# An adaptive layer-norm block on one core: W_up turned by VectorE and DMAs in place of TensorE, the first modulation's columns made directly, and some copies moved between engines

## The reference

```python
mod = (silu(c) @ wmod).reshape(4, 6, 1, 512)       # sa, ca, ga, sb, cb, gb
ga, gb = sign(ga) * max(abs(ga), 0.25), the same of gb
h = layernorm(x) * (1 + ca) + sa
q, k, v = split(h @ Wqkv + bqkv)                   # 512 -> 3 x 128
x = x + ga * (softmax(q k^T / sqrt(128)) v @ Wo + bo)
h = layernorm(x) * (1 + cb) + sb
top1 = argmax(h @ gate_w^T + expert_bias)
ffn = h @ W_up^T + lora_B[top1] @ (lora_A[top1] @ h)
out = x + gb * ffn
```

## Time and profile before

| | |
|---|---|
| median of 3 runs | 181.64 us (181.44 to 181.71) |
| the profiled execution: its own time | 181.46 us |
| its span, first to last instruction | 179.7 us |
| granted TensorE clock, mean | 1.000 |
| busy: TensorE / its weight loads | 170.8 us (95%) / 134.0 us (75%) |
| busy: VectorE / ScalarE / GpSimd | 139.4 (78%) / 90.1 (50%) / 80.4 us (45%) |
| share of the last-ending chain: PE / DVE / POOL / ACT / issue / DMA | 68 / 10 / 7 / 6 / 5 / 2% |
| W_up's 16 transposes on TensorE (L658) | 1.91 us busy |
| W_up's high parts on ScalarE (L932), low parts on VectorE (L1303), 4 each | 2.06 us, 2.48 us |

### The profile page before, as it was taken

The page is one execution under the profiler, slowest core; times in us unless marked ns, Lnnn a source line. Parts: engine busy times, 40 slices in busy tenths (PEclk is TensorE's granted clock), DMA queues, the critical chain, the costliest instruction groups (busy, mean ns, idle before and its releaser), DMA issues.

```text
span 179.7 us, 2828 instructions
## 1 busy us (share of the span) xinstructions
PE 170.8 (95%) x918; PEld 134.0 (75%) x918; DVE 139.4 (78%) x352; ACT 90.1 (50%) x170; POOL 80.4 (45%) x109
## 2 busy tenths in 40 slices
PE   6889999989999999999999999999999999999990
PEld 5755757878678788878867787888887878768890
DVE  1957859998969997969999839699298275989964
ACT  3375045964278894339349651713477502583100
POOL 3464201279334549041979950019694000452550
PEclk9999999999999999999999999999999999999999
DMA  4999997930041002353031753001140000001414
GB/s 160 378 387 387 387 387 145 385 106 9 0 168 71 0 2 73 96 125 122 0 117 58 201 136 75 0 0 58 60 158 22 0 2 0 0 4 58 175 48 185
DMA packets 13902, 21.32 MB, mean 119 GB/s; under 512 B 3340, under 2 KB 4112, under 8 KB 13888
## 3 DMA queue, kind: packets, MB, share of 16 engines
q1 hardware_dynamic: 13888, 21.15, 35.3%
HBM read 14.83 MB, written 4.21 MB: 106 GB/s over the span
## 4 chain that ended last, share of the span: by engine, by line
PE 68%; DVE 10%; POOL 7%; ACT 6%; issue 5%; DMA 2%; SPq 0%; POOLq 0%; DVEq 0%; ACTq 0%
PE bank L398 44%; PE bank L412 3%; PE bank L521 3%; DVE stats L1020 2%; PE bank L548 2%; DMA xs<-in_L_attn_x_dram 2%; PE bank L506 2%; ACT xn_p L845 2%; PE bank L500 2%; PE bank L572 2%; PE bank L574 2%; PE bank L503 2%; POOL rstd L1493 1%; POOL xs L1508 1%; DVE xs L1232 1%
## 5 line engine op out<-in xcount | busy, mean ns | idle before, releaser
L398 PE MATMUL bank<-wup_lo,h2hi 128*128 128x512 f32 (+1 forms) x68 | 27.3, 401 | 0.4 <-ACT h2hi L903 0.4
L884 ACT ACTIVATE xn_p<-xs,shift,rstd 128x512 f32<-128x512 f32 x16 | 13.1, 816 | 26.1 <-POOL shift L1496 26.0
L398 PE MATMUL bank<-wup_hi,h2hi 128*128 128x512 f32 (+1 forms) x68 | 25.9, 381 | 0.0
L398 PE MATMUL bank<-wup_hi,h2lo 128*128 128x512 f32 (+1 forms) x68 | 25.9, 381 | 0.0
L1493 POOL TENSOR_TENSOR rstd<-var_eps,neg_half 128x1 f32<-128x1 f32 x16 | 8.8, 552 | 37.1 <-DVE var_eps L1243 37.1
L1508 POOL TENSOR_TENSOR xs<-xs,f_gb 128x512 f32<-128x512 f32 x14 | 17.9, 1292 | 7.7 <-DVE f_gb L1297 7.7
L398 PE MATMUL bank<-h1lo,wqkv_hi 128*128 128x512 f32 x48 | 19.6, 409 | 0.7 <-DVE modT_ca L1074 0.7
L1485 POOL TENSOR_TENSOR xs<-xs,gabo 128x512 f32<-128x512 f32 x16 | 20.3, 1306 | 0.1
L398 PE MATMUL bank<-h1hi,wqkv_hi 128*128 128x512 f32 x48 | 19.0, 395 | 0.0
L398 PE MATMUL bank<-h1hi,wqkv_lo 128*128 128x512 f32 x48 | 18.9, 394 | 0.0
L1215 DVE TENSOR_TENSOR plo<-bank,phi 128x512 fp32r<-128x512 f32 x16 | 10.0, 685 | 6.7 <-ACT phi L853 6.6
(11 more groups left out here) (185 smaller groups left out, 408.7 us busy)
## 6 DMA issues: line engine op xcount, KB each, us to landing
out_dram<-xs SPq DMA_DIRECT2D x15, 256.0 KB, 2.0
stage<-in_L_wmod_dram SPq DMA_DIRECT2D x3, 1024.0 KB, 7.3
xs<-in_L_wmod_dram SPq DMA_DIRECT2D x3, 1024.0 KB, 9.5
xs<-in_L_attn_x_dram SPq DMA_DIRECT2D x3, 1024.0 KB, 7.8
stage<-xn SPq DMA_DIRECT2D x32, 64.0 KB, 2.1
xs<-in_L_attn_x_dram SPq DMA_DIRECT2D x2, 512.0 KB, 3.8
f_gb<-in_L_ffn_W_up_dram SPq DMA_DIRECT2D x1, 1024.0 KB, 11.3
gb_bc<-gates_dram SPq DMA_DIRECT2D x4, 256.0 KB, 4.2
```

Source lines behind the costliest of these rows:

```text
L398: mm = nc.tensor.matmul(dst, w, m, start=first and i == 0, stop=last and i == total - 1)
L884: nc.scalar.activation(xn2_p[:, t, :], xs[:, b, t, :], ACT.Identity, bias=shift[:, 1, t:t + 1], scale=rstd[:, 1, t:t + 1]).then_inc(S["xn2 ...
```

## The change

It has three parts.

1. **W_up.** It is loaded into `xs[:, 2]` once modulation 1 has read section sa there, ahead of section sb. VectorE turns its 32x32 blocks from `xs[:, 2]` to `f_gb` (`turn_wup`, four instructions spread between its steps of batch 0); SP moves the blocks by 16 DMAs from `f_gb` to `stage` (`move_wup`); ScalarE makes the high parts from `stage`; GpSimd makes the low parts, two before batch 0's second layer-norm deviations and two behind them. The x rows of batch 2 are loaded into `xs[:, 2]` only when all four turns are done, section cb goes into `f_gb` and is loaded only when the 16 moves have landed, and `move_turned(2)` waits for W_up's parts. TensorE's 16 transposes and VectorE's 4 subtractions are gone. VectorE's statistics of batch 2, tiles 0 and 1, stand where the subtractions stood.
2. **Section ca.** TensorE makes the four column tiles of ca directly, each by four products of 128x128 weights (the section) and 4 columns (silu(c)); the four side-by-side products, VectorE's copy of the rows, four transposes and three products of the identity are gone. VectorE takes all four tiles' statistics of batch 0 before the steps of silu.
3. **Copies moved.** Two of the four tiles of batch 1's first normalisation go from VectorE to ScalarE (GpSimd makes their offsets), and both `gate_rows_evacuate` go from VectorE to ScalarE. Banks 1 and 5 change places in the plan, so that `pv(0)` no longer opens the bank that held ga's rows.

```diff
-        (2, "x1T", 1, 0), (4, "x1T", 1, 1), (6, "x1T", 1, 2), (7, "x1T", 1, 3), (5, "O", 0),
-        (2, "wupT", 0), (4, "wupT", 1), (6, "wupT", 2), (7, "wupT", 3),
-        (1, "qkv", 1, 0), (3, "qkv", 1, 1), (0, "qkv", 1, 2),
-        (5, "Y", 0, 0), (4, "Y", 0, 1), (6, "Y", 0, 2), (7, "Y", 0, 3), (2, "mod", 3),
-        (5, "gateA"), (4, "loraB"), (2, "modT", 3),
-        (6, "x2T", 0, 0), (7, "x2T", 0, 1), (5, "x2T", 0, 2), (4, "x2T", 0, 3),
+        (2, "x1T", 1, 0), (4, "x1T", 1, 1), (6, "x1T", 1, 2), (7, "x1T", 1, 3), (1, "O", 0),
+        (5, "qkv", 1, 0), (3, "qkv", 1, 1), (0, "qkv", 1, 2),
+        (1, "Y", 0, 0), (4, "Y", 0, 1), (6, "Y", 0, 2), (7, "Y", 0, 3), (2, "mod", 3),
+        (1, "gateA"), (4, "loraB"), (2, "modT", 3),
+        (6, "x2T", 0, 0), (7, "x2T", 0, 1), (1, "x2T", 0, 2), (4, "x2T", 0, 3),
     ]
-    m, f = (2, 1, 3, 0, 6), (5, 7, 4)
+    m, f = (2, 5, 3, 0, 6), (1, 7, 4)
...
+        wup_blocks = f_gb[:].rearrange("p t h -> p (t h)").rearrange("p (a k t i) -> p a k t i", a=NB, k=NK, t=NK)
+        wup_turned = stage[:].rearrange("p t h -> p (t h)").rearrange("p (c k t i) -> p c k t i", c=NB, k=NK, t=NK)
...
-        raw = {"ca": stage[:], "sa": xs[:, 2], "ga": xs[:, 3], "sb": stage[:], "cb": stage[:], "gb": xs[:, 3],
-               "wup": f_gb, "wqkv": xn2_p}
+        raw = {"ca": stage[:], "sa": xs[:, 2], "ga": xs[:, 3], "sb": stage[:], "cb": f_gb[:], "gb": xs[:, 3],
+               "wup": xs[:, 2], "wqkv": xn2_p}
...
             def wait_used(g):
-                sp.wait_ge(S["mod_psum"], g + 1)
+                if g == 0:
+                    sp.wait_ge(S["ca_psum"], NK)
+                else:
...
+
+            def move_wup():
+
+                for a in range(NB):
+                    for c in range(NB):
+                        sp.dma_start(wup_turned[a * BLOCK:(a + 1) * BLOCK, c].rearrange("p k t i -> p (k t i)"),
+                                     wup_blocks[c * BLOCK:(c + 1) * BLOCK, a].rearrange("p k t i -> p (k t i)")
+                                     ).then_inc(wup_moved, 16)
...
             sp.dma_start(xs[:, 1], x_v[1]).then_inc(x_in[1], 16)
             load_section("ga")
+            wait_used(1)
+            sp.dma_start(raw["wup"], wup.rearrange("(o p) h -> p o h", p=P)).then_inc(wup_in, 16)
             wait_used(0)
             load_section("sb")
-            wait_used(1)
-            sp.dma_start(xs[:, 2], x_v[2]).then_inc(x_in[2], 16)
             sp.dma_start(wo_raw[:], wo).then_inc(wo_in, 16)
             sp.dma_start(bo_bc[:], bo.partition_broadcast(P)).then_inc(bo_in, 16)
-            sp.dma_start(raw["wup"][:], wup.rearrange("(o p) h -> p o h", p=P)).then_inc(wup_in, 16)
...
+            sp.wait_ge(S["wup_blocks_turned"], NK)
+            sp.dma_start(xs[:, 2], x_v[2]).then_inc(x_in[2], 16)
             wait_used(2)
+            load_section("gb")
+            move_wup()
+            write_gate(0)
+            sp.wait_ge(wup_moved, 16 * NB * NB)
             load_section("cb")
-            load_section("gb")
-            write_gate(0)
             spread_gate(0, 1)
             wait_used(3)
             sp.dma_start(xs[:, 3], x_v[3]).then_inc(x_in[3], 16)
+            sp.wait_ge(S["wup_hi_ready"], NK)
+            sp.wait_ge(S["wup_lo_ready"], NK)
             move_turned(2, (0, 1))
             write_gate(1)
             move_turned(2, (2, 3))
...
-            def first_modulation_columns(half):
-                pe.wait_ge(S["mod_rows_ready"], half + 1)
-                dst = open_bank("caT", half)
-                for nt in (2 * half, 2 * half + 1):
-                    mm = nc.tensor.transpose(dst[:, nt * P:(nt + 1) * P], mod_rows[:, 0, nt * P:(nt + 1) * P], ident[:])
-                mm.then_inc(S["modT_psum"], 1)
+            def first_modulation_columns(nts):
+
+                pe.wait_ge(mod_in["ca"], 16)
+                pe.wait_ge(S["silu_step"], 4)
+                for nt in nts:
+                    dst = open_bank("ca", nt)
+                    for kt in range(NK):
+                        mm = nc.tensor.matmul(dst[:, 0:B], raw["ca"][:, kt, nt * P:(nt + 1) * P], silu_wide[:, kt, 0:B],
+                                              start=kt == 0, stop=kt == NK - 1)
+                    mm.then_inc(S["ca_psum"], 1)
...
-            def w_up_transposes(kts):
-                pe.wait_ge(wup_in, 16)
-                for kt in kts:
...
-            keep_warm(bank[5], 3)
+            first_modulation_columns((0,))
+            first_x1_transposes((2, 3))
+            first_modulation_columns((1, 2, 3))
             qkv(0, (0,))
             modulation(1)
...
-            w_up_transposes(range(NK))
...
+            def second_ln1_normalise():
+                act.wait_ge(S["x1T_psum"], NK)
+                for t in range(NT - BY_ACT_1, NT):
+                    act.wait_ge(S["ln1_shift"], BY_ACT + t - (NT - BY_ACT_1) + 1)
+                    nc.scalar.activation(xn1[:, t, :], xs[:, 1, t, :], ACT.Identity, bias=shift[:, 0, t:t + 1],
+                                         scale=rstd[:, 0, t:t + 1]).then_inc(S["xn1_by_act"], 1)
+
...
+            def gate_rows_evacuate(s):
+                i = ("ga", "gb").index(s)
+                act.wait_ge(S["gate_row_psum"], i + 1)
+                nc.scalar.activation(gates[:, i, :], at("gate_row", s)[0:B, :], ACT.Copy).then_inc(S["gates_ready"], 1)
+
             def wup_high(kts):
                 for kt in kts:
-                    act.wait_ge(S["wupT_psum"], kt + 1)
-                    nc.scalar.activation(wup_hi[:, kt, :], at("wupT", kt)[:], ACT.Copy).then_inc(S["wup_hi_ready"], 1)
+                    act.wait_ge(wup_moved, 16 * NB * NB)
+                    nc.scalar.activation(by_rows(wup_hi[:, kt, :]), wup_turned[:, :, kt], ACT.Copy).then_inc(S["wup_hi_ready"], 1)
...
+            second_ln1_normalise()
...
             wo_high(0)
             h1_high(1, (2, 3))
+            gate_rows_evacuate("ga")
             o_high(0)
...
                 pt_high(b)
+                if b == 1:
+                    gate_rows_evacuate("gb")
...
+            def first_columns(nts):
+
+                for nt in nts:
+                    dve.wait_ge(S["ca_psum"], nt + 1)
+                    nc.vector.tensor_scalar(modT["ca"][:, nt, :], at("ca", nt)[:, 0:B], 1.0, None,
+                                            ALU.add).then_inc(S["modT_ready"], 1)
...
-            def gate_rows_evacuate(s):
-                i = ("ga", "gb").index(s)
-                dve.wait_ge(S["gate_row_psum"], i + 1)
-                nc.vector.tensor_copy(gates[:, i, :], at("gate_row", s)[0:B, :]).then_inc(S["gates_ready"], 1)
...
-            def wup_low(kts):
-                for kt in kts:
-                    dve.wait_ge(S["wup_hi_ready"], kt + 1)
-                    nc.vector.tensor_tensor(wup_lo[:, kt, :], at("wupT", kt)[:], wup_hi[:, kt, :].bitcast(F32),
-                                            ALU.subtract).then_inc(S["wup_lo_ready"], 1)
+            def turn_wup(tiles):
+                dve.wait_ge(wup_in, 16)
+                for t in tiles:
+                    nc.vector.transpose(wup_blocks[:, :, :, t],
+                                        raw["wup"][:, t, :].rearrange("p (k a i) -> p a k i", k=NK, a=NB)
+                                        ).then_inc(S["wup_blocks_turned"], 1)
...
-            ln1_stats(0, (0,))
-            first_ln1_aggregate(0)
-            first_ln1_variance(0)
+            for t in range(NT):
+                ln1_stats(0, (t,))
+                first_ln1_aggregate(t)
+                first_ln1_variance(t)
...
-            for t in range(1, NT):
-                ln1_stats(0, (t,))
-                first_ln1_aggregate(t)
-                first_ln1_variance(t)
             first_ln1_normalise()
-            first_modulation_rows()
-            first_columns(0)
+            first_columns((0, 1, 2))
             h1_low(0, (0,))
-            first_columns(1)
+            first_columns((3,))
             h1_low(0, (1, 2, 3))
             ln1_stats(1, (0, 1, 2, 3))
             ln1_moments(1)
             add_parts("sa")
             widen_sa()
-            second_ln1_normalise()
+            second_ln1_normalise((0,))
             qkv_shift_row()
+            turn_wup((0,))
+            second_ln1_normalise((1,))
             qkv_shift()
+            turn_wup((1,))
             qk_low(0)
-            ln1_stats(2, (0, 1))
+            turn_wup((2, 3))
...
-            gate_rows_evacuate("ga")
             h1_low(1)
             split_sb()
             inverse_sums(0)
             o_low(0)
-            wup_low(range(NK))
+            ln1_stats(2, (0, 1))
...
-                if b == 1:
-                    gate_rows_evacuate("gb")
...
+            def wup_low(kts):
+                for kt in kts:
+                    pool.wait_ge(S["wup_hi_ready"], kt + 1)
+                    nc.gpsimd.tensor_tensor(by_rows(wup_lo[:, kt, :]), wup_turned[:, :, kt], by_rows(wup_hi[:, kt, :].bitcast(F32)),
```

(4 more changed lines are left out.)

80 lines of the change are left out of this document (32 added, 48 removed).

## The result

| | before | after |
|---|---|---|
| median of 6 runs, us | 181.68 (181.44 to 182.41) | 185.25 (185.01 to 186.37) |
| ratio after / before, 95% | | 1.0203 (1.0177 to 1.0228) |
| profiled execution, us | 181.46 | 185.01 |
| its span, us | 179.7 | 183.3 |
| mean granted clock, profiled execution | 1.000 | 0.977 |

What follows compares the result with a forecast made beforehand. TensorE bounds the prologue and steady part, other engines' lines batch 0's second layer norm and batch 1. Profiled 181.46 less 0.7 gives 180.8; with the median 0.18 above that execution, forecast 180.9 us, own range 180.0 to 181.9, eight in ten 179.5 to 183.0.

Steps and rivals of the forecast that it cites:

- The start, +0.3: Prologue: ca's 32 loads at 0.11 us put `qkv(0)` at about 14.2 instead of 13.89, +0.3 us (-0.4 to +1.1).
- a dear start of +1.1: Rival, prologue: at 0.138 us per load the start costs 1.1 us instead of 0.3, total 181.7; chance 0.13.
- sb, 0 with 0.4 to spare: Before modulation 2: sb, loaded behind W_up, lands at 25.5, modulation 2 is reached at 25.9; cost 0.
- VectorE's turns, 0: VectorE in batch 0: W_up's four turns of 0.69 us replace two normalisations and two statistics there; cost 0.
- P by V without its wait: Batch 0's product of P and V: no 0.70 us wait for ga's rows, start at 36.35 instead of 36.66.
- First line, the moves and cb: Before modulation 3: cb lands at 47.6 behind the 16 moves, TensorE waits 1.2 us; 0.7 of 2.0 gained is left.
- the rival of m over 0.70: Rival, SP's moves: from 0.70 us per issue (m) cb makes modulation 3 later than before; 0.78 gives 182.9; chance 0.20.
- Second line, GpSimd: Batch 0's second layer norm: two low parts of 1.27 us, deviations from 47.6; allows VectorE's modulation 3 sum at 53.76 - 0.9.
- the rival of 1.5 times: Rival, GpSimd: low parts at 1.5 times 1.27 us make that line 1.3 later and decisive, total 182.0; chance 0.12.
- Batch 1 and later: From 53.76: the 0.7 us gain reaches SP's moves, ga's broadcast and 94.17; gb's rows on ScalarE cost 0.

Runs made afterwards that it cites:

- e1_start_only: The kernel before with only the start changed (ca's columns made directly, VectorE's order): 184.3 us, ratio 1.0166.
- e2_no_start: The changed kernel with the start of the kernel before; W_up's part and the moved copies stay: 181.73 us, ratio 1.0000.
- e5_no_start_cb_early: As `e2_no_start`, but cb is loaded right behind the moves' issue, into the buffer of the first layer norm's rows: 181.84 us, ratio 1.0010.
- e6_low_late: As `e5_no_start_cb_early`, with GpSimd's first two low parts behind batch 0's deviations, the last two behind batch 2's offsets: 181.45 us, ratio 0.9982.
- e10_low_last: As `e6_low_late`, with all four low parts of W_up behind batch 2's offsets on GpSimd: 183.83 us, ratio 1.0078.
- e14_no_hold: As `e6_low_late`, with two VectorE instructions in other forms and batch 1's `gabo` behind VectorE's gate columns: 181.02 us, ratio 1.0000.
- e14b_repeat: `e14_no_hold` run once more, unchanged: 181.48 us, ratio 0.9991.
- e11_gpsimd_adds: The kernel before with two GpSimd additions of 128x512, behind batch 0's deviations, into a buffer nobody reads: 181.94 us, ratio 1.0021.
- e17_low_behind_scaling: As `e14_no_hold`, with GpSimd's first two low parts of W_up waiting for VectorE's scaling of cb's columns: 181.56 us, ratio 0.9978.

## Why the prediction was wrong, step by step

- *The start, +0.3.* The terms were good: 0.11 us per load (2.74 us for 24 in `e1_start_only`), first tile at 9.5, first `qkv` product at 14.2 (9.53 and 14.29). **This is the step that failed**, by what it left out: that TensorE, at a mean clock of 1.000 in before, stays there through 16 products of four columns. It didn't, and the work behind them ran at half the clock. In `e1_start_only` modulation 2 came 1.8 late, 1.5 of it in the slow stretch, and with ca landing 1.1 later, as in after, 4.5 late. My rivals had a dear start of +1.1 by dear loads, none by a lower clock.
- *sb, 0 with 0.4 to spare.* 0.24 late in after, 0.25 to 1.63 in `e2_no_start`, `e5_no_start_cb_early`, `e6_low_late`, `e10_low_last`, `e14_no_hold` and `e14b_repeat`. An estimate by mean speed and one landing could not carry a margin of 0.4.
- *VectorE's turns, 0.* Right: 0.70 us each, and the last ends ahead of the first maximum.
- *P by V without its wait.* Right (a wait of 0.21 for P's low part), by the bank.
- *First line, the moves and cb.* The sixteen issues took 10.80 us, 0.675 each (10.15 in `e2_no_start`), so the rival of m over 0.70 didn't come. Modulation 3 came behind an idle 1.52 us in place of the 1.2 forecast. Two errors nearly cancel in this: the first move went out 3.3 us behind modulation 2's start and not 4.6, since the issue of batch 2's rows took 0.37 and not 1.37, and the last move landed 4.0 us after its issue and not 2.1.
- *Second line, GpSimd.* 1.27 us for each low part, as forecast; the rival of 1.5 times fell. Where sb was on time this line ended as forecast: VectorE's sum of modulation 3 at 52.98 in `e5_no_start_cb_early` (53.76 - 0.9 = 52.86). In `e2_no_start` it is at 54.16, with sb's wait of 1.63 in it. But the line did not end at this sum: when the low parts run beside it, they hold the scaling behind it up by 0.2 to 1.0 us. In after this scaling is free, since TensorE's wait for cb let GpSimd finish at 57.76, just ahead of it.
- *Batch 1 and later.* What is gained at batch 1's scores reached the span less 0.3 to 0.5 us in `e2_no_start`, `e5_no_start_cb_early`, `e6_low_late` and `e14_no_hold`. It goes near 96 us, where TensorE waits 0.5 us for VectorE's `qk_lo`; `e1_start_only` and `e11_gpsimd_adds` show this wait too, and I have no cause for it.

No version here beats the kernel before by more than the measurement can tell. The best, `e6_low_late`, `e14_no_hold` and `e17_low_behind_scaling`, stand at ratios of 0.998 to 1.000.
